# The sync engine holds back context, stores, x and expert weights until a row of maxima has landed

## The chip, the cores and the metric

The kernel runs on one core of one Trainium2 chip. Its time is the device time in microseconds of one execution.
## The reference

32 batches of 112 tokens (width 256) attend with 16 heads to a context of 375 rows, and then pass a mixture of 8 experts of which each token takes 2:

```python
x = x + tanh(g_xattn[0]) * xattn(layernorm(x), ctx, ctx, Wq, bq, Wk, bk, Wv, bv, Wo, bo)
x = x + tanh(g_ffn[0]) * ffn(layernorm(x), w_router, w1, w2, w3)

# xattn: softmax(Q K^T / sqrt(16)) V per head, then Wo, bo
# ffn: scores = softmax(xf @ w_router.T); the 2 best experts of a token;
#      y_e = (silu(xf @ w1[e]) * (xf @ w3[e])) @ w2[e]; sum of score * y_e over the two
```

The context comes in transposed (features first). All is float32; matrix operands are kept as float32r in a few places.

## The kernel before

**Attention** is a pipeline over batches. Every engine runs a loop over `i` from -3 to 31 (SP to 32), and in turn `i` works on several batches at once: exponentials of batch `b = i`, maxima of the scores of `c = i + 1`, value projection of `s = i + 2`, key and query projection of `a = i + 3`, the output projection of `e = i - 1` and the second layer norm of `r = i - 2`. A turn has 12 places `k`, one for each of the 12 score tiles (`exps`, line 1130).

The softmax needs the row maxima before the exponentials. `maxes` (line 1162) computes the scores of batch `c` into PSUM, VectorE takes the negated maxima (line 869), TensorE turns them (`negmax_turn`, line 1178), ScalarE copies them to SBUF (line 645), and GpSimd sends them with two small DMAs (`nm_rows`, line 389) into row 96 of `stack`, as an extra row of the matmul operand. This is done in two halves: half 0 of batch `i + 1` at `k = 5` of turn `i`, needed by `exps` at `k = 0` of turn `i + 1`; half 1 of batch `i` at `k = 1` of turn `i`, needed at `k = 6` of the same turn. `s_nmrow[half][batch % 3]` counts 32 for each pair that has landed. The other user of it is line 644: ScalarE does not overwrite the copied maxima before the send of the batch before has landed.

**The sync engine.** In turn `i`, SP first waits for the low half of the keys of batch `i + 2` (line 298) and then issues 16 DMAs that build that batch's `stack` (lines 280 to 286); the maxima of that batch read it from `k = 0` of turn `i + 1`. Behind them it issues what the turn has left: the context of batch `i + 4` (line 221, read by the key projection at `k = 2` of turn `i + 1`), the store of the attention result of batch `i - 2` (242) and of its norm for batch `i - 3` (248), now and then four batches of x (228), in turns 1 to 6 copies that fill `xn_dram` (320), from turn 3 on expert weights (325). Then it goes on to turn `i + 1`. Turn 1 also fills the table of tokens and some spare rows (315 to 318). SP's order is the order of the code.

**The end of attention.** In turn 30 (`i == LAST - 2`) SP has no stack to build. It issues two stores and then `first_weights` (line 256): 16 transfers of the upper half of `w3` (8, line 261) and of the first rows of `w2` (8, line 263), into memory that `split` and `stack` held. The `n`-th of them waits until `exps` of batch 30 has done `3n/4 + 1` of its 12 tiles (line 258). Then come four `load_idx` (253: the token numbers of the first four expert tiles, read from a table in DRAM), and in turn 31 two stores, the rest of `w2` (line 337, 1024 and 768 KB) and the numbers of 12 more tiles.

**The experts** are 63 tiles of up to 128 tokens. GpSimd gathers a tile's rows by its numbers (`gather`, line 496; the first four in turn 31), TensorE turns them (`turn_rows`, 1361), multiplies by `w1` and `w3` (`inner`, 1417), turns the hidden tile (1436) and multiplies by `w2` (1478); GpSimd adds the result into `out` (505). TensorE waits for the first gathered tile at `k = 10` of turn 31 (line 1337), and for all of `w2` before its first use (line 1472). Tiles turn, gather and add in order of their number.

Of the kernel before, what the change touches and what calls it, by code (L numbers as in the profile page):

```python
# [6 lines left out]
def flamingo(nc, x, ctx_kv, g_xattn, g_ffn, Wq, bq, Wk, bk, Wv, bv, Wo, bo, w_router, w1, w2, w3, out):  # L7
# [4 lines left out]
    B, SQ, EMB = x.shape  # L12
# [12 lines left out]
    NSLOT = 3  # L25
    NX = 16
    GB = 4
    NG = B // GB

    NE, _, F = w1.shape  # L30
    TOK = B * SQ
    TOP = 2
# [15 lines left out]
    with ctx, late:  # L48
# [3 lines left out]
        def sem(name):  # L52
            return ctx.enter_context(nc.semaphore(name))
# [77 lines left out]
        s_nmrow = [[sem(f"s_nmrow{h}{n}") for n in range(NSLOT)] for h in range(2)]  # L131
# [52 lines left out]
        def placed(n, g):  # L184
            return 16 * TOP * sum(len(UNITS[u]) for u in range(g, n, 2))

        def wait(eng, s, v):
            if v > 0:
                eng.wait_ge(s, v)  # L190

        def place_of(n):
            return (n - B) % NSLOT
# [6 lines left out]
        def stacked(n):  # L200
            return 256 * (n // NSLOT + 1) - (96 if n % NSLOT == 0 else 0)

        def live(n):
            return n if 0 <= n < B else None
# [13 lines left out]
        def _(sp):  # L218
            def load_ctx(b):
                wait(sp, s_v_ps, KC * (b - NSLOT + 1))  # L220
                sp.dma_start(ctx_t[:, b % NSLOT, :, :], ctx_kv[b, :, :].rearrange("(c p) s -> p c s", p=P)).then_inc(s_ctx[b % NSLOT], 16)

            def load_x(g):
                if g >= 4:
                    wait(sp, s_xn2, GB * (g - 3))
                    for n in range(GB):
                        wait(sp, s_x2st[n], 16 * (g - 3))
                sp.dma_start(xa[:, GB * g % NX:GB * g % NX + GB, :], x[GB * g:GB * g + GB, :, :].rearrange("b q d -> q b d")).then_inc(s_x[g % 4], 16)
# [11 lines left out]
            def store_x2(b):  # L240
                wait(sp, s_st2, b + 1)
                sp.dma_start(out[SQ * b:SQ * b + SQ, :], xrow(b)).then_inc(s_x2st[b % GB], 16)

            def store_xn2(r):
                if r == GB * (SNAP + 1):
                    sp.wait_ge(s_spare, SPARE)
                sp.wait_ge(s_xn2 if r < B - 1 else s_xn2_end, min(r + 1, B - 1) if r < B - 1 else 1)
                sp.dma_start(xn_dram[SQ * r:SQ * r + SQ, :], xn2[:, r % GB, :]).then_inc(s_xn2st[r % GB], 16)

            def load_idx(t):  # L250
                at = sp.value_load(s_idx[0:1, t:t + 1], min_val=0, max_val=ROWS // P - 1)
                wait(sp, s_idx_in[t % NIS], 16 * (t // NIS))
                sp.dma_start(idx[:, t % NI, :], table.rearrange("(t p) c -> t p c", p=P)[bass.ds(at, 1), :, :].rearrange("t p c -> p (t c)")
                             ).then_inc(s_idx_in[t % NIS], 16)

            def first_weights():
                for n in range(2 * NE):
                    sp.wait_ge(s_exp_ps, 12 * (B - 2) + 3 * n // 4 + 1)
                    e = n % NE
                    if n < NE:  # L260
                        sp.dma_start(w3_hi[:, e, :], w3[e, P:2 * P, :]).then_inc(s_w13, 16)
                    else:
                        sp.dma_start(w2_sb[:, 0, e, :], w2[e, 0:P, :]).then_inc(s_w2, 16)

            for i in range(FIRST, LAST + 1):
                s, a = live(i + 2), live(i + 3)
                if i == LAST - 2:
                    sp.wait_ge(s_map, 1)
                    for g in range(2):
                        sp.wait_ge(s_scat[g], placed(SNAP + 1, g))  # L270
                    sp.sem_inc(s_met_sp, 1)
                if s is not None:
                    if s < 2:
                        sp.wait_ge(s_split0, 1)
                    wait(sp, s_exp_ps, 12 * (s - NSLOT + 1))
                    src, dst = split[:, s % 2, :, :].bitcast(f32), stack[:, place_of(s), :, :].bitcast(f32)

                    def from_high(g):
                        rows, pr = slice(32 * g, 32 * g + 32), slice(DC * g, DC * g + DC)
                        sp.dma_start(dst[0:32, pr, 0:SKP], src[rows, :, KHI:KHI + SKP]).then_inc(s_stack[s % NSLOT], 16)  # L280
                        sp.dma_start(dst[0:32, pr, SKP:KQ], src[rows, :, QHI:QHI + QW]).then_inc(s_stack[s % NSLOT], 16)

                    def from_low(g):
                        rows, pr = slice(32 * g, 32 * g + 32), slice(DC * g, DC * g + DC)
                        sp.dma_start(dst[32:64, pr, :], src[rows, :, KLO:KLO + KQ]).then_inc(s_stack[s % NSLOT], 16)
                        sp.dma_start(dst[64:96, pr, :], src[rows, :, KHI:KHI + KQ]).then_inc(s_stack[s % NSLOT], 16)

                    if s == 0:
                        sp.wait_ge(s_qlo, 1)
                        sp.wait_ge(s_khi, DC)  # L290
                        for g in range(3):
                            from_high(g)
                        sp.wait_ge(s_klo, DC)
                        for g in range(2):
                            from_low(g)
                    else:
                        wait(sp, s_klo, DC * (s + 1))
                        sp.sem_inc(s_met_sp, 1)
                        wait(sp, s_qlo, s + 1)
                        for g in range(4):  # L300
                            from_high(g)
                            from_low(g)
                if a is not None and NSLOT - 1 <= a < B - 1:
                    load_ctx(a + 1)
                if live(i - 2) is not None:
                    store_x2(i - 2)
                if live(i - 3) is not None:
                    store_xn2(i - 3)
                if i == -1:
                    load_x(2)  # L310
                if i == 2:
                    load_x(3)
                if i == 1:
                    sp.wait_ge(s_pad, 2)
                    sp.dma_start(table.rearrange("(p n) c -> p (n c)", n=256), pad_tab[:, :, :, :].rearrange("p a b c -> p (a b c)")).then_inc(s_tab0, 16)
                    for n in range(DC):
                        sp.dma_start(out[TOK:TOK + P, P * n:P * n + P], ident[:, :]).then_inc(s_spare, 16)
                        sp.dma_start(xn_dram[TOK:TOK + P, P * n:P * n + P], ident[:, :]).then_inc(s_spare, 16)
                for n in range(GB * (SNAP + 1) + 2 * i - 2, GB * (SNAP + 1) + 2 * i) if 1 <= i <= (B - GB * (SNAP + 1)) // 2 else ():
                    sp.dma_start(xn_dram[SQ * n:SQ * n + SQ, :], x[n, :, :]).then_inc(s_spare, 16)  # L320
                if i == 3:
                    sp.wait_ge(s_tab0, 16)
                for n in (2 * i - 6, 2 * i - 5) if 3 <= i < 8 else (i + 2,) if 8 <= i < 22 else ():
                    src, dst, h = ((w1, w1_sb[:, 0], 0), (w1, w1_sb[:, 1], 1), (w3, w3_lo, 0))[n // NE]
                    sp.dma_start(dst[:, n % NE, :], src[n % NE, P * h:P * h + P, :]).then_inc(s_w13, 16)
                if i >= 7 and i % GB == 3 and (i + 9) // GB < NG:
                    load_x((i + 9) // GB)
                if i == LAST - 2:
                    sp.wait_ge(s_stack[(B - 1) % NSLOT], stacked(B - 1))
                    first_weights()  # L330
                    for t in range(4):
                        load_idx(t)
                if i == LAST - 1:
                    sp.wait_ge(s_nmrow[1][(B - 1) % NSLOT], 32 * ((B - 1) // NSLOT + 1))
                    for c in range(1, FC):
                        n = min(P, F - P * c)
                        sp.dma_start(w2_sb[0:n, c, :, :], w2[:, P * c:P * c + n, :].rearrange("e p d -> p e d")).then_inc(s_w2, 16)
                    for t in range(4, NI):
                        load_idx(t)
# [1166 lines left out]
```

## Time and profile before

| | us |
|---|---|
| median of 3 runs | 856.07 (853.0 to 857.51) |
| the profiled execution, its own time | 855.32 |
| its span in the trace | 853.6 |
| busy in the span: PE / PEld / DVE / ACT / POOL | 825.3 / 673.7 / 486.3 / 422.2 / 476.2 |
| mean granted clock of TensorE | 0.991 of full speed |

The attention takes the span up to about 570 us, the expert tiles the rest. A busy PE is not PE at its peak, since the ends of matmuls are modelled; whether PE is what others wait for is to be read from the chain of waits and from the idle time in front of its lines. A row of a timeline gives the start, the duration, the engine and the line; SPq is the sync engine's queue, and its duration is that of the issue, not of the transfer. In brackets stands the idle time ahead of an instruction and who ended it. "To landing" is the time from an issue to the last write. A turn of attention takes about 16.9 us.

### The profile page before, as it was taken

How to read it: one execution, taken by the hardware profiler on the slowest of the kernel's cores; microseconds unless marked ns; L12 is line 12 of the kernel's file. 1: busy time of each engine (PE TensorE's matmuls, PEld its weight loads, DVE VectorE, ACT ScalarE, POOL GpSimd, SP SyncE). 2: the span in 40 equal slices, each digit the busy share in tenths (PEclk: the TensorE clock that was granted, in tenths of full speed). 3: DMA queues.
4: the chain of work that ended last, by engine and by line, in shares of the span. 5: the costliest groups of instructions: out<-in, count | busy, mean ns of one | idle time of the engine just before them, and what ended most of it. 6: DMA issues, size and time to landing. Idle time of an engine off the chain costs nothing.

```text
span 853.6 us, 21453 instructions
## 1 busy us (share of the span) xinstructions
PE 825.3 (97%) x7209; PEld 673.7 (79%) x7209; DVE 486.3 (57%) x1163; ACT 422.2 (49%) x1086; POOL 476.2 (56%) x570
## 2 busy tenths in 40 slices
PE   7899999999999999999999999899999999999995
PEld 6578888888888888888888888777777777777773
DVE  4566776777777776777787777655622222222221
ACT  2256665665666566656665666565222222222221
POOL 6454434454555555555655465455777766656652
PEclk8999999999999999999999999999999999999997
DMA  5876777776676677676656664574444443444432
GB/s 153 207 161 168 204 177 174 180 192 156 161 181 155 158 175 172 148 175 164 170 117 158 150 160 111 146 192 74 57 63 62 70 69 62 63 63 63 63 57 31
DMA packets 99842, 112.29 MB, mean 132 GB/s; under 512 B 29276, under 2 KB 81124, under 8 KB 99736
## 3 DMA queue, kind: packets, MB, share of 16 engines
q1 hardware_dynamic: 79720, 92.48, 45.1%
q0 software_dynamic: 18512, 17.60, 13.5%
q8 instruction: 61, 1.00, 0.6%
q10 hardware_dynamic: 1504, 0.85, 0.5%
q14 instruction: 45, 0.37, 0.2%
HBM read 35.48 MB, written 17.53 MB: 62 GB/s over the span
## 4 chain that ended last, share of the span: by engine, by line
PE 85%; DVE 11%; issue 2%; ACT 1%; DMA 1%; POOLq 0%; DVEq 0%; ACTq 0%
PE ps L1417 18%; PE ps L1173 10%; PE ps L1478 10%; PE ps L1162 9%; PE ps L1145 9%; PE ps L1130 8%; DVE negmax L869 6%; PE ps L1168 5%; PE ps L1273 3%; PE ps L1332 3%; PE ps L1436 2%; PE ps L1361 2%; PE ps L1265 2%; PE ps L1247 1%; DVE xa L854 1%
## 5 line engine op out<-in xcount | busy, mean ns | idle before, releaser
L869 DVE TENSOR_REDUCE negmax<-ps 112x2 f32<-112x750 f32 x256 | 240.1, 940 | 124.3 <-PE ps L1162 122.8
L594 ACT ACTIVATE probs<-ps 125x448 f32<-125x448 f32 x384 | 209.5, 547 | 101.8 <-PE ps L1130 95.6
L389 POOL DMA_DIRECT2D stack<-negmax_t x128 | 68.2, 536 | 228.5 <-ACT negmax_t L645 220.8
L1130 PE MATMUL ps<-stack 97*125 97x224 f32 x768 | 189.1, 328 | 0.9 <-ACT probs L594 0.4
L1130 PEld LDWEIGHTS ps<-stack 97*125 97x125 f32 x768 | 127.4, 188 | 28.1 <-ACT probs L594 1.5
L1162 PE MATMUL ps<-stack 96*112 96x376 f32 x512 | 136.7, 348 | 7.7 <-DVE negmax L869 5.4
L505 POOL DMA_INDIRECT out_dram<-y,idx x63 | 100.5, 1595 | 69.5 <-issue 34.4
L689 ACT ACTIVATE silu<-ps 128x352 f32<-128x352 f32 x63 | 29.3, 465 | 184.4 <-PE ps L1417 184.4
L1081 DVE TENSOR_TENSOR h<-silu,ps 128x352 f32<-128x352 f32 x63 | 32.8, 521 | 144.6 <-PE ps L1417 144.4
L1168 PE MATMUL ps<-wv_sb,ctx_t 128*125 128x256 f32 x384 | 100.0, 382 | 0.4 <-DVE split L859 0.4
L1173 PE MATMUL ps<-ctx_t,wk_sb 128*128 128x375 f32 x256 | 93.7, 489 | 0.7 <-ACT q_raw L654 0.7
L1478 PE MATMUL ps<-w_sb,h_t 128*128 x378 | 92.3, 380 | 0.7 <-ACT h_t L695 0.7
L1478 PEld LDWEIGHTS ps<-w_sb,h_t 128*128 128x128 f32 x378 | 71.7, 190 | 20.1 <-issue 0.9
L1417 PE MATMUL ps<-w_sb,xg_t 128*128 x252 | 84.9, 458 | 0.0
L1162 PEld LDWEIGHTS ps<-stack 96*112 96x112 f32 x512 | 72.0, 177 | 15.0 <-DVE negmax L869 13.9
L1145 PE MATMUL ps<-probs,v_sb 125*17 125x112 f32 x3072 | 79.8, 260 | 0.0
L1145 PEld LDWEIGHTS ps<-probs,v_sb 125*17 125x17 f32 x3072 | 71.7, 98 | 8.0 <-ACT probs L594 5.4
L496 POOL DMA_INDIRECT xg<-xn_scratch,idx x63 | 62.5, 992 | 25.4 <-issue 17.2
L567 ACT ACTIVATE v_sb<-ps 125x256 f32<-125x256 f32 x96 | 36.5, 381 | 78.8 <-PE ps L1145 76.6
L409 POOL DMA_INDIRECT slot_table<-pay,slots_i x64 | 64.2, 1003 | 15.3 <-issue 13.6
L1168 PEld LDWEIGHTS ps<-wv_sb,ctx_t 128*125 128x125 f32 x384 | 66.6, 187 | 6.8 <-DVE split L859 0.6
L1173 PEld LDWEIGHTS ps<-ctx_t,wk_sb 128*128 128x128 f32 x256 | 46.7, 195 | 18.3 <-issue 1.7
(221 smaller groups left out, 1216.9 us busy)
## 6 DMA issues: line engine op xcount, KB each, us to landing
stack<-split SPq DMA_DIRECT2D x252, 150.0 KB, 2.7
ctx_t<-in_ctx_dram SPq DMA_DIRECT2D x32, 375.0 KB, 3.9
stack<-split SPq DMA_DIRECT2D x127, 94.0 KB, 2.5
stack<-split SPq DMA_DIRECT2D x127, 56.0 KB, 2.1
out_dram<-xa SPq DMA_DIRECT2D x32, 112.0 KB, 3.5
xn_scratch<-xn SPq DMA_DIRECT2D x32, 112.0 KB, 3.3
xa<-in_x_dram SPq DMA_DIRECT2D x7, 448.0 KB, 5.6
w_sb<-in_L_ffn_w_dram SPq DMA_DIRECT2D x16, 176.0 KB, 3.1
```

The lines of the kernel that those rows point to most:

```text
L389: gp.dma_start(dst[:, :, SKP + SQ * h:SKP + SQ * h + SQ], negmax_t[4 * h:4 * h + 4, half, :].bitcast(f32)).then_inc(s_nmrow[half][c % NSLO ...
L409: gp.indirect_dma_start(table, bass.IndirectOffsetOnAxis(ap=slots_i[:, u % 2, GB * k + j:GB * k + j + 1], axis=0), pay[:, UNITS[u][j], k, ...
L505: gp.indirect_dma_start(out, bass.IndirectOffsetOnAxis(ap=idx[:, t % NI, 0:1], axis=0), y[:, t % NY, :], None, compute_op=ALU.add).then_in ...
L594: act.activation(probs[:, n % NP, :], ps[0:KW, EXPB + k % 2, 0:4 * SQ], ACT.Exp).then_inc(s_exp, 1)
L869: dve.tensor_reduce(negmax[:, half, :, p4], ps[0:SQ, m1:m2 + 1, 0:SK], axis=AX.X, op=ALU.max, negate=True).then_inc(s_max, 1)
L1130: last = pe.matmul(ps[0:KW, EXPB + k % 2, QW * m:QW * m + QW], stack[:, place_of(b), p, KW * ch:KW * ch + KW], stack[:, place_of(b), p, SK ...
L1145: last = pe.matmul(ps[32 * j:32 * j + HD + 1, PVB, SQ * g:SQ * g + SQ], v_sb[:, b % NSLOT, ch, head, :], probs[:, (12 * b + 3 * g + ch) % ...
L1162: last = pe.matmul(ps[0:SQ, max_banks(c, t)[h], 0:SKP], stack[0:ONE_ROW, place_of(c), t, SKP + SQ * h:SKP + SQ * h + SQ], stack[0:ONE_ROW, ...
L1168: last = pe.matmul(ps[0:KW, bank, 0:EMB], ctx_t[:, s % NSLOT, n, KW * ch:KW * ch + KW], wv_sb[:, n, :], start=(n == 0), stop=(n == DC - 1))
L1173: last = pe.matmul(ps[:, bank, 0:SK], wk_sb[:, n, P * m:P * m + P], ctx_t[:, a % NSLOT, n, :], start=(n == 0), stop=(n == DC - 1))
L1417: last = pe.matmul(ps[:, bank, 0:F], xg_t[:, t % NS, k, :], w[k][:, bass.ds(e, 1), :].rearrange("p e f -> p (e f)"), start=(k == 0), stop= ...
L1478: last = pe.matmul(ps[:, YB, 0:EMB], h_t[0:n, c, :], w2_sb[0:n, c, bass.ds(e_o, 1), :].rearrange("p e d -> p (e d)"), start=(c == 0), stop ...
```

## The change

One wait is added to the sync engine's loop, in turns 0 to 30, between the stack transfers and everything else that the turn issues:

```diff
                         for g in range(4):
                             from_high(g)
                             from_low(g)
+                if 0 <= i < B - 1:
+                    sp.wait_ge(s_nmrow[0][(i + 1) % NSLOT], 32 * ((i + 1) // NSLOT + 1))
                 if a is not None and NSLOT - 1 <= a < B - 1:
                     load_ctx(a + 1)
                 if live(i - 2) is not None:
```

The semaphore is that of half 0 of batch `i + 1`. No instruction is added besides, none is removed and none changes its place in a stream. So the order of every engine is as before, and only what an instruction waits for differs. On the sync engine, from the stores of turn 29 to the first of the weights, before:

```order
L242 DMA out_dram<-xa 112x256 [waits s_st2]
L248 DMA xn_scratch<-xn 112x256 [waits s_xn2]
L242 DMA out_dram<-xa 112x256 [waits s_scat1,s_map,s_scat0,s_st2]
L248 DMA xn_scratch<-xn 112x256 [waits s_xn2]
L261 DMA w_hi<-in_L_ffn_w_dram 128x352 [waits s_exp_ps,s_stack1]
```

And the same place now:

```order
L242 DMA out_dram<-xa 112x256 [waits s_st2,s_nmrow00]
L248 DMA xn_scratch<-xn 112x256 [waits s_xn2]
L242 DMA out_dram<-xa 112x256 [waits s_scat1,s_map,s_scat0,s_st2,s_nmrow01]
L248 DMA xn_scratch<-xn 112x256 [waits s_xn2]
L261 DMA w_hi<-in_L_ffn_w_dram 128x352 [waits s_exp_ps,s_stack1]
```

The first row stands behind the stack of turn 29 and the third opens turn 30; `s_nmrow01` is half 0 of batch 31. The same wait stands in front of the context load (line 221) of turns 0 to 27.

## Rows read from the trace of the kernel before

**Rows 1.** The page: the chain that ended last by engine, and line 1130 with its idle time.
```profile
PE 85%; DVE 11%; issue 2%; ACT 1%; DMA 1%; POOLq 0%; DVEq 0%; ACTq 0%
...
L1130 PE MATMUL ps<-stack 97*125 97x224 f32 x768 | 189.1, 328 | 0.9 <-ACT probs L594 0.4
```

**Rows 2.** Timeline, sync engine, one step: start us, us, engine, line, what.
```profile
309.90 0.59 SPq L280 DMA_DIRECT2D stack<-split  x1
...
315.04 1.87 SPq L280 DMA_DIRECT2D stack<-split  x1
...
320.79 0.60 SPq L286 DMA_DIRECT2D stack<-split  x1
321.43 0.59 SPq L221 DMA_DIRECT2D ctx_t<-in_ctx_dram  x1
...
323.08 0.43 SPq L325 DMA_DIRECT2D w_lo<-in_L_ffn_w_dram  x1
326.74 0.61 SPq L280 DMA_DIRECT2D stack<-split  x1
```

**Rows 3.** Timeline, GpSimd, in the same step: the two sends of maxima.
```profile
321.58 1.06 POOL L389 DMA_DIRECT2D stack<-negmax_t  x2 [3.40 <-ACT negmax_t L645]
```

**Rows 4.** Line 389 alone, 321.0 to 321.8 us: time to landing.
```profile
DMA to landing us min/median/max: 3.8/3.8/3.8
```

**Rows 5.** DMA issues, 312 to 329.7 us: KB each, median us to landing.
```profile
stack<-split SPq DMA_DIRECT2D x9, 150.0 KB, 2.7
...
ctx_t<-in_ctx_dram SPq DMA_DIRECT2D x1, 375.0 KB, 4.1
```

**Rows 6.** Timeline, TensorE, the start of the next step.
```profile
328.97 0.46 PE L1130 MATMUL ps<-stack 97*125 97x224 f32 x2
329.55 0.60 PE L1162 MATMUL ps<-stack 96*112 96x376 f32 x2
...
333.32 1.43 PE L1173 MATMUL ps<-ctx_t,wk_sb 128*128 128x375 f32 x4
```

**Rows 7.** Timeline, GpSimd, loop turn 3: the two sends of maxima.
```profile
101.64 1.09 POOL L389 DMA_DIRECT2D stack<-negmax_t  x2 [4.71 <-ACT negmax_t L645]
```

**Rows 8.** Timeline, sync engine, first stack transfers of turns 4 and 5.
```profile
106.82 0.65 SPq L280 DMA_DIRECT2D stack<-split  x1
...
123.66 0.65 SPq L280 DMA_DIRECT2D stack<-split  x1
```

**Rows 9.** Timeline, GpSimd, the end of attention.
```profile
555.97 1.07 POOL L389 DMA_DIRECT2D stack<-negmax_t  x2 [2.03 <-PE ps L1130]
...
564.61 1.08 POOL L496 DMA_INDIRECT xg<-xn_scratch,idx  x1 [0.17 <-issue]
```

**Rows 10.** Line 389 alone, 555.9 to 557 us: time to landing.
```profile
DMA to landing us min/median/max: 2.7/2.8/2.9
```

**Rows 11.** Timeline, sync engine, the end of attention.
```profile
547.68 6.72 SPq L261 DMA_DIRECT2D w_hi<-in_L_ffn_w_dram  x8
555.37 4.22 SPq L263 DMA_DIRECT2D w_sb<-in_L_ffn_w_dram  x8
560.66 4.83 SPq L253 DMA_DIRECT2D idx<-slot_table  x4
...
566.48 1.26 SPq L337 DMA_DIRECT2D w_sb<-in_L_ffn_w_dram  x2
```

**Rows 12.** The same, 548.2 to 549.5 us alone: two issues.
```profile
548.11 0.93 SPq L261 DMA_DIRECT2D w_hi<-in_L_ffn_w_dram  x2
```

**Rows 13.** Timeline, TensorE, first expert tile turned, first use of w2.
```profile
569.81 0.38 PE L1361 MATMUL ps<-ident,xg 128*128 128x128 f32 x2
...
580.45 1.54 PE L1478 MATMUL ps<-w_sb,h_t 128*128 x6
```

**Rows 14.** DMA issues, 561 to 590 us: KB each, us to landing.
```profile
w_sb<-in_L_ffn_w_dram SPq DMA_DIRECT2D x1, 768.0 KB, 12.3
```

**Rows 15.** Stretches: us, busy us of PE, PEld, DVE, ACT, POOL, PEclk, DMA.
```profile
12.00:16.00 4.00, 3.63 (x11) 2.88 (x12) 0.28 (x1) 0.82 (x3) 0.80 (x2) 0.50 0.57 121
```

## The prediction

> **What bounds the kernel now.** I read the page first: the chain of waits that ended last and the costliest lines. The reader is to see that TensorE holds 85% of the chain, VectorE 11% and DMA 1% [rows 1]. The new wait is for a DMA that brings maxima to line 1130, so the second thing to see is the idle time in front of that line: 0.9 us in the whole run, and ended by ScalarE, not by a transfer [rows 1]. No maxima are late now. Then I read the sync engine's timeline, once in the middle of the attention and once at its end, and beside it the sends of the maxima and the readers on TensorE. The end matters because there the sync engine's stream holds something else: the first expert weights, the first token numbers, the rest of w2.
>
> **The added wait in a common turn.** A turn takes 16.84 us, from the stack's first transfer at 309.90 to the next batch's at 326.74 [rows 2]. The stack's 16 issues last to 321.43; then come context, two stores and one weight slice, done at 323.51, and the engine stands idle for 3.2 us [rows 2]. GpSimd sends half 0 at 321.58, two DMAs in 1.06 us, so the second starts at about 322.1 [rows 3], and it takes 3.8 us to land [rows 4]. The wait therefore ends at 325.9 at the latest. What is queued behind it takes 323.51 - 321.43 = 2.1 us, and is out at 328.0: the next stack starts 1.3 us later than 326.74. Who waits for that?
>
> - The context, issued at 325.9 with 4.1 us to landing [rows 5], is there at 330.0. The key projection reads it at 333.32 [rows 6]. Spare: 3.3 us.
> - The stack's last issue, at 320.79 now, lands 2.7 us later at 323.5 [rows 2, 5]; the maxima read it at 329.55 [rows 6]. 6.1 us of spare, 4.8 us after the shift.
> - The sync engine itself: 328.0 plus 11.5 us for the stack (321.43 - 309.90) is 339.5, and the next maxima land at 325.9 + 16.84 = 342.7. It does not fall behind from turn to turn.
> - Stores, x and weights have readers that are at least a turn away.
>
> So I cost the wait at nothing in common turns; what hides it is the 3.2 us in which the sync engine is idle anyway and the 3.3 us by which the context is early. In turn 3 seven DMAs are held (context, two stores, two copies, two weight slices), 7 x 0.53 = 3.7 us at the pitch of the four above. The sends start at 101.64 [rows 7], the second lands at about 102.2 + 3.8 = 106.0, the seven are out at 109.7, and the stack of turn 4 starts 2.9 us after its 106.82 [rows 8]. Of 6.1 us of spare 3.2 us are left. Turns 4 to 6 are alike, turn 1 holds eight small ones.
>
> Does it gain anything? The maxima would no longer have the context transfer beside them. They might land in 2.8 us, as at the end of attention [rows 10], instead of 3.8 us. But they land at 325.9 now and are read at 328.97 [rows 6]; earlier is worth nothing. And the turn with more traffic is not longer: from turn 4 to 5, with two copies and two slices in it, the stack starts are 123.66 - 106.82 = 16.84 us apart [rows 8], as in the middle [rows 2]. The Trainium skill says, in "DMA: Bandwidth & Descriptors", section "Issuing engines are not separate DMA queues", that transfers of all engines interleave on the same 16 DMA engines; by that rule alone holding back the context should speed up the maxima, and the sum would be a gain of up to 1 us a turn if somebody waited for them. The two landing times (3.8 and 2.8 us) agree with it, and the 0.9 us of idle time says that nobody waits.
>
> **The added wait in turn 30.** Here the cover is gone. There is no stack in this turn, so the sync engine comes to the wait early. The sends of half 0 of batch 31 start at 555.97 [rows 9]; the second at 556.5, and it lands 2.8 us later [rows 10], at 559.3. Now the w3 transfers are spread from 547.68 to 554.4 and those of w2 from 555.37 to 559.59, paced by the score tiles, and the first token numbers are issued at 560.66, 1.07 us after the last of them [rows 11]. With the wait, two stores and 16 transfers start at 559.3 together. The pacing no longer delays them, but each issue costs: two in 0.93 us, or 0.48 us each with the gap [rows 12]. 18 x 0.48 = 8.6, so they are out at 567.9, and the first numbers are issued at 569.0, 8.3 us later than now. With no w3 traffic beside them the maxima will land sooner than in 2.8 us; I take off 0.5 us, a choice, and have a shift of 7.8 us for all that follows on the sync engine. Two readers are on the path:
>
> - The first gather. It starts at 564.61 [rows 9], and TensorE turns its tile at 569.81 [rows 13]: at most 5.2 us from gather to tile. The trace does not show its landing, and 2.7 us, a plain transfer's [rows 5], is the least I allow. The numbers issued at 568.5 land 2.7 us later, so the gather starts at about 571.4 and the tile is there between 574.1 and 576.6. TensorE loses 4.3 to 6.8 us.
> - The rest of w2. The second of its two transfers is issued at about 567.2 [rows 11] and takes 12.3 us [rows 14], to 579.5; its first use is at 580.45 [rows 13]. The margin is 0.9 us. Shifted by 7.8 us, it makes TensorE 6.9 us late, the first loss included.
>
> The later of the two decides: 6.9 us. Behind it nothing gives it back, since the expert tiles are TensorE's work back to back. Sum against the profiled execution: 855.3 + 0 (30 turns) + 6.9 = 862.2 us. The median of the three runs is 0.7 us above that execution, well within what they differ by.
>
> The ends of this term: at the pitch of a stack issue, 0.64 us [rows 2], the 18 take 2.9 us more, and a stretched issue such as that of 1.87 us [rows 2] adds 1.3 us, so 866 is reachable; the shift cannot be under what the gather allows with the fastest landing, 3.6 us.
>
> **Rivals.**
>
> - *The tail costs less.* The 12.3 us of w2 are so long because gathers, stores and number loads run beside it [rows 14]; if those are spread differently, w2 arrives sooner, and only the gather counts: 4.3 us less the 0.7 us that the maxima may land earlier, 3.6 us, 858.9 us. For it: margins of a microsecond decide. Against: all its neighbours shift with it.
> - *The clock.* TensorE will stand still for over 4 us, and then 10.6 us of work lie before the first use of w2 (580.45 - 569.81). After the first waits of the kernel the granted clock was 0.50 over 12 to 16 us, the level of 1.2 GHz [rows 15]. If 4 us at that level follow the stop, 2 us are lost, less what the wait for w2 hides (0 to 2.6 us): up to 864.2 us. The Trainium skill, "TensorE: Matmul & The Clock Gate", Part 1, says that an idle array falls back to half rate; what it gives here is that time, and no stop so long is in the attention of this trace.
> - *Slower in the attention.* In turns 1 and 3 to 6 the spare is down to 3.2 us by my count, and the held transfers (about 1.2 MB) lie directly ahead of the stack in the queue. If they cost 5 us instead of 3, TensorE loses 2 us in each of five turns: 872 us. It decides once a stack lands over 6.1 us later than now.
> - *Faster.* A common turn gets shorter because no bulk transfer is beside the maxima, by 0.4 us in each of 30 turns: 12 us, less the tail, 850 us. It decides if line 1130 or its ScalarE readers wait for landings that the trace puts down to others. Against it stand the 0.9 us of idle time and the equal turns.
> - That the wait does nothing is excluded by the rows: the engine reaches it at 321.43, and the landing is at 325.9.
>
> **Chances.** Forecast 0.52 (859.5 to 866), less tail 0.20, clock 0.09, slower attention 0.06, faster 0.13. What a measurement can tell from no change is 0.5%, 4.3 us. Slower by more than that: the forecast, clock and attention, and 0.03 of the less costly tail, 0.70. Within it: the rest of that case, 0.17. Faster: 0.13. The range of 856.5 to 866.5 leaves out the faster case, a little of the cheap tail, and the slow attention. Slower holds most, and the forecast's own range is 859.5 to 866.
>
> **What would show it.** Right: the turns stay at 16.8 us and the context load starts at the landing of the maxima; the w3 and w2 transfers of turn 30 stand in one block from about 559 to 568; the first numbers are issued near 568.5; line 1361 has 4 to 7 us of idle time, ended by the gather, and line 1478 perhaps 1 to 2 us before its first use. Wrong: idle time in front of line 1162 or 1173 ended by a DMA in the attention, or a block of 16 transfers that is out before 565, or turns under 16.6 us.

## The result and the profile after

| | before | now |
|---|---|---|
| median of 6 runs, us | 856.79 (853.0 to 858.1) | 862.96 (862.31 to 865.86) |
| ratio of the times, 95% interval | | 1.0091 (1.006 to 1.0122) |
| the profiled execution, its span, us | 855.32, 853.6 | 862.31, 860.6 |
| mean granted clock of TensorE | 0.991 | 0.990 |

The kernel is slower by 0.9%, or 6.2 us of the medians. The forecast was 862.2 us.

The page first: the shares of the chain, and the line that reads the maxima.

```profile
PE 84%; DVE 11%; issue 2%; DMA 2%; ACT 1%; SPq 0%; ACTq 0%; POOLq 0%; POOL 0%; DVEq 0%
...
L1132 PE MATMUL ps<-stack 97*125 97x224 f32 x768 | 189.3, 329 | 2.9 <-DMA stack<-negmax_t 2.1
```

Against [rows 1] TensorE has one point less and DMA one more, and line 1132 (1130 before) now waits 2.9 us instead of 0.9, ended by the landing of maxima. The waits of the sync engine (total us, times, longest) show where the added wait acts:

```profile
SPq L221 <- DMA stack<-negmax_t: 69.8, 28, 5.0
SPq L298 <- DVE split L861: 19.2, 19, 2.3
SPq L242 <- DMA stack<-negmax_t: 15.5, 3, 11.3
```

28 waits in front of the context and 3 in front of line 242, the longest of them 11.3 us: that one is turn 30. A common turn now, on the sync engine:

```profile
318.04 0.60 SPq L286 DMA_DIRECT2D stack<-split  x1
321.44 0.40 SPq L221 DMA_DIRECT2D ctx_t<-in_ctx_dram  x1
...
322.85 0.46 SPq L327 DMA_DIRECT2D w_lo<-in_L_ffn_w_dram  x1
324.49 0.61 SPq L280 DMA_DIRECT2D stack<-split  x1
```

This turn stands 2.25 us earlier in the trace than the one of [rows 2], for a reason that lies at the start of the kernel and is told below. The context goes out 3.4 us after the stack's last issue began, and the next stack starts at 324.49. With 2.25 added that is 326.74, the very time of [rows 2]: it is not late at all. Over turns 2 to 27 the context goes out 2.1 to 3.4 us after the first send of half 0 (once 4.6 us), and in turns 3 to 8 the next stack starts 0.7 to 1.7 us later than before. From the first value matmul of turn 1 to that of turn 30 the attention takes 489.85 us now and took 489.88 before.

From there to the end it is 313.83 us instead of 304.56, 9.3 us more. First the sync engine at the end of the attention, then GpSimd, then the landing of GpSimd's second pair of sends, those of half 1 of batch 31:

```profile
555.86 0.33 SPq L242 DMA_DIRECT2D out_dram<-xa  x1
556.24 0.42 SPq L248 DMA_DIRECT2D xn_scratch<-xn  x1
556.76 3.74 SPq L261 DMA_DIRECT2D w_hi<-in_L_ffn_w_dram  x8
560.54 4.95 SPq L263 DMA_DIRECT2D w_sb<-in_L_ffn_w_dram  x8
566.55 3.68 SPq L253 DMA_DIRECT2D idx<-slot_table  x4
...
571.22 1.30 SPq L339 DMA_DIRECT2D w_sb<-in_L_ffn_w_dram  x2
```

```profile
553.70 1.07 POOL L391 DMA_DIRECT2D stack<-negmax_t  x2 [2.03 <-PE ps L1132]
...
559.77 1.03 POOL L391 DMA_DIRECT2D stack<-negmax_t  x2 [3.62 <-ACT negmax_t L647]
...
569.99 1.08 POOL L498 DMA_INDIRECT xg<-xn_scratch,idx  x1 [7.81 <-DMA idx<-slot_table]
```

```profile
DMA to landing us min/median/max: 4.3/5.0/5.7
```

For comparison the same pair in the kernel before:

```profile
DMA to landing us min/median/max: 1.9/2.4/2.8
```

The two stores and the 16 weight transfers stand in one block from 555.86 to 565.5, the first numbers follow at 566.55, and the gather waits 7.81 us for them. New is what the landings show: the pair sent at 559.77, behind w3 and beside w2, lands after 4.3 to 5.7 us instead of 1.9 to 2.8. TensorE, the readers and the first use of w2, and the landing of its last part:

```profile
566.01 0.70 PE L1132 MATMUL ps<-stack 97*125 97x224 f32 x4 [2.11 <-DMA stack<-negmax_t]
...
573.42 0.41 PE L1363 MATMUL ps<-ident,xg 128*128 128x128 f32 x2 [2.46 <-DMA xg<-xn_scratch,idx]
...
578.90 3.42 PE L1147 MATMUL ps<-probs,v_sb 125*17 125x112 f32 x96
...
587.61 1.54 PE L1480 MATMUL ps<-w_sb,h_t 128*128 x6
```

```profile
w_sb<-in_L_ffn_w_dram SPq DMA_DIRECT2D x1, 768.0 KB, 12.2
```

TensorE stands still twice, 2.11 us for the maxima and 2.46 us for the first gathered tile; in front of its first use of w2, at 587.61, it does not wait. The last part of w2, issued at about 571.9, landed at 584.1. And the stretches of this place (columns as in [rows 15]):

```profile
560.00:566.00 6.00, 3.43 (x76) 2.72 (x64) 3.30 (x18) 2.40 (x5) 2.14 (x4) 1.00 1.00 342
566.00:570.00 4.00, 3.77 (x15) 2.97 (x16) 0.18 (x2) 2.46 (x6) 0.01 (x1) 0.65 0.27 74
570.00:574.00 4.00, 1.54 (x11) 1.18 (x10) 1.25 (x4) 0.68 (x2) 3.09 (x4) 0.92 0.58 163
574.00:578.00 4.00, 3.90 (x17) 2.36 (x15) 0.65 (x5) 2.44 (x7) 3.35 (x4) 0.50 1.06 309
578.00:582.00 4.00, 3.72 (x94) 3.27 (x98) 0.00 (x0) 0.41 (x1) 0.63 (x1) 0.64 0.97 180
```

The granted clock is 0.50 to 0.92 from 566 to 582 us; in the trace of before every stretch from 549 to 600 has 1.00. Both kernels take the same 253.60 us from a later point to the end (from 607.00 now, from 600.00 before), so the 9.3 us arise ahead of it. The stretches from the value matmuls of turn 30 to that point, now and before:

```profile
546.77:607.00 60.23, 52.98 (x520) 41.21 (x520) 25.85 (x92) 29.51 (x65) 29.81 (x31) 0.91 0.49 117
```

```profile
549.04:600.00 50.96, 48.59 (x521) 38.57 (x521) 25.93 (x93) 29.43 (x65) 29.67 (x31) 1.00 0.59 133
```

The same work (520 and 521 recorded matmuls) takes 60.23 us instead of 50.96. TensorE is busy 52.98 us of it instead of 48.59: 4.4 us more for the same instructions, at a clock of 0.91. The other 4.9 us are more idle time.

These two sums do not say which stop decides, and the order of events does. The first tile is turned 26.65 us after turn 30's value matmuls (573.42 - 546.77) and was turned 20.77 us after them before (569.81 - 549.04): 5.9 us late. The tile hangs on the numbers, and these on the sync engine's issues, which do not wait for half 1. So the stop of 2.11 us, and the lower clock of the stretch behind it, lie inside this lateness: without them TensorE would have waited longer for the same tile. From the tile to the first use of w2 it is then 14.19 us instead of 10.64, 3.5 us more, with TensorE busy for 13.81 us of them at a mean granted clock of 0.76. These two terms, 5.9 and 3.5 us, make the 9.3, give or take 0.1.

Against these 9.3 us stand 2.3 us that were won before turn 1. The added wait is first met in turn 0, so it has no part in them. The first rows of TensorE's timeline, now and before:

```profile
1.61 9.15 PE L1119 MATMUL ps<-ident 128*128 128x128 f32 x56 [1.61 <-POOL ident L366]
...
13.31 2.70 PE L1175 MATMUL ps<-ctx_t,wk_sb 128*128 128x375 f32 x8
```

```profile
1.61 7.99 PE L1117 MATMUL ps<-ident 128*128 128x128 f32 x56 [1.61 <-POOL ident L364]
...
14.18 4.95 PE L1173 MATMUL ps<-ctx_t,wk_sb 128*128 128x375 f32 x8
```

The same 56 warm-up matmuls took 9.15 us in this execution and 7.99 us in the other, so that TensorE stood still for 0.65 us behind them here and for 1.81 us there; the first 8 key projections then took 2.70 us at a granted clock of 1.00, and 4.95 us at the 0.50 of [rows 15]. Executions differ there without an edit, as the runs below show (with the same warm-up the value matmuls of turn 1 start between 56.9 and 59.8 us). So 7.0 us between the two spans are 9.3 lost at the end of the attention less 2.3 won at the start.

### The profile page after: what moved, and what is told of

Same layout as the page of the kernel before. It is cut to its first block, busy times and chain, and to the rows that moved or that the text cites. A ratio compares the mean times of both kernels' runs of the same rounds, so it can differ in the third digit from the quotient of the medians.

```text
span 860.6 us, 21484 instructions
## 1 busy us (share of the span) xinstructions
PE 827.7 (96%) x7209; PEld 675.7 (79%) x7209; DVE 486.3 (57%) x1163; ACT 422.1 (49%) x1086; POOL 476.1 (55%) x570
## 3 DMA queue, kind: packets, MB, share of 16 engines
q0 software_dynamic: 18512, 17.60, 12.8%
## 4 chain that ended last, share of the span: by engine, by line
PE 84%; DVE 11%; issue 2%; DMA 2%; ACT 1%; SPq 0%; ACTq 0%; POOLq 0%; POOL 0%; DVEq 0%
PE ps L1419 17%; PE ps L1480 10%; PE ps L1164 9%; PE ps L1175 9%; PE ps L1147 9%; PE ps L1132 8%; DVE negmax L871 6%; PE ps L1170 5%; PE ps L1275 3%; PE ps L1334 3%; PE ps L1438 2%; PE ps L1363 2%; PE ps L1267 1%; PE ps L1249 1%; DVE xa L856 1%
## 5 line engine op out<-in xcount | busy, mean ns | idle before, releaser
L1175 PE MATMUL ps<-ctx_t,wk_sb 128*128 128x375 f32 x256 | 91.5, 479 | 0.7 <-ACT q_raw L656 0.7
L1419 PEld LDWEIGHTS ps<-w_sb,xg_t 128*128 128x128 f32 x252 | 47.9, 191 | 17.2 <-issue 0.5
```

The lines of the kernel that those rows point to most:

```text
L1175: last = pe.matmul(ps[:, bank, 0:SK], wk_sb[:, n, P * m:P * m + P], ctx_t[:, a % NSLOT, n, :], start=(n == 0), stop=(n == DC - 1))
L1419: last = pe.matmul(ps[:, bank, 0:F], xg_t[:, t % NS, k, :], w[k][:, bass.ds(e, 1), :].rearrange("p e f -> p (e f)"), start=(k == 0), stop= ...
```

## The experiments

In all of them "the wait" is the added one. Turn lengths are the distances between the first value matmuls of neighbouring turns; "the tail" is the time from turn 30's to the end of the span, 304.56 us before and 313.83 now. Unless an edit says otherwise it is made to the changed kernel.

**The wait in turns 0 to 29 alone**, and **in turn 30 alone**:

```diff
-                if 0 <= i < B - 1:
+                if 0 <= i < B - 2:      # the first kernel
+                if i == B - 2:          # the second
```

> The added wait stands in turns 0 to 29 only. Theory (all of the loss is made in turn 30, the wait in a common turn is hidden): no change, ratio 1.000 within 0.002; the turns after turn 2 stay at 16.85 to 17.15 us as in the kernel before, and from the value matmuls of turn 30 to the end of the span it is 304.6 us as before. Rival 1 (the wait shortens common turns, and the changed kernel got its 2.27 us lead at turn 30 from it): about 2 us faster than before, ratio 0.997. Rival 2 (late stack transfers cost in turns 3 to 6): turns over 17.2 us there.

> The added wait stands in turn 30 only. Theory: it makes the whole loss; from the value matmuls of turn 30 to the end of the span 313.8 us as in the changed kernel, against 304.6 us before, and a ratio of 1.009 like the whole change. Rival (the wait of common turns costs or gains too): the ratio differs from that of the whole change by over 0.002.

Measured: turns 0 to 29 alone 856.68 us (12 runs, 855.01 to 859.32; ratio to before 1.0011, 0.9997 to 1.0024), attention 489.79 us, tail 305.87. Turn 30 alone 862.96 us (6 runs, 860.79 to 866.18; ratio 1.0086, 1.0063 to 1.0108), attention 489.80 us, tail 313.19. So thirty of the 31 waits cost nothing that can be told from noise, and the last one costs all. The tail of the first is 1.3 us over the 304.6 expected: TensorE waits 1.16 us there for the second gathered tile. The same stop, 0.81 us, stands in the kernel before with more warm-up (below), which has no added wait. With turn 30's wait alone TensorE stands still at the same two places:

```profile
568.02 1.07 PE L1132 MATMUL ps<-stack 97*125 97x224 f32 x4 [1.70 <-DMA stack<-negmax_t]
...
575.49 0.66 PE L1363 MATMUL ps<-ident,xg 128*128 128x128 f32 x2 [2.10 <-DMA xg<-xn_scratch,idx]
```

**The first numbers ahead of the weights**, with the full wait. The four `load_idx` of turn 30 go in front of `first_weights`:

```diff
-                    first_weights()
                     for t in range(4):
                         load_idx(t)
+                    first_weights()
```

> The whole change, but in turn 30 the first four token-number loads are issued ahead of the 16 weight transfers, right behind the wait. Theory (three things make the 9.3 us: half 1 of batch 31's maxima behind the weight block, 2.1 us; the late gather, 2.5 us of idle time; the clock that falls after them): the gather starts before 565 us, the wait for it is gone, that of 2.1 us before line 1132 stays or grows by up to 1 us, since the weight block is later by the four number loads of 1.2 us each; total loss 3 to 6 us against before. Rival (the rest of w2 binds behind the gather, as the prediction had it): the loss stays near 7 us, with idle time ahead of the first use of w2.

Measured: 863.25 us (4 runs, 862.37 to 865.29; ratio 1.0095, 1.0072 to 1.0118), tail 313.92. The sync engine, the landing of half 1, and TensorE's idle time over 1 us:

```profile
558.56 4.25 SPq L253 DMA_DIRECT2D idx<-slot_table  x4
562.85 3.78 SPq L261 DMA_DIRECT2D w_hi<-in_L_ffn_w_dram  x8
```

```profile
DMA to landing us min/median/max: 1.9/2.3/2.7
```

```profile
571.95 1.45 PE L1419 MATMUL ps<-w_sb,xg_t 128*128 x4 [2.24 <-DMA w_hi<-in_L_ffn_w_dram]
...
586.74 2.76 PE L1480 MATMUL ps<-w_sb,h_t 128*128 x6 [3.67 <-DMA w_sb<-in_L_ffn_w_dram]
```

The gather starts at 563.16 and no reader of maxima waits, but nothing is won. The half-1 pair, sent at 560.58 with no weight ahead of it, lands in 2.3 us. TensorE then waits 2.24 us for w3, which is issued 5.3 us later than in the changed kernel (15.27 us behind the first value matmul of turn 30 instead of 9.99), and 3.67 us for the last part of w2. The expectation had the stop for half 1 staying and a loss of 3 to 6 us; both were wrong, and its rival, the rest of w2, was right. The first tile is turned 20.77 us after turn 30's value matmuls, just as before.

**The same, and the first part of w2 after half 1.** In `first_weights`:

```diff
+                    if n == NE:
+                        sp.wait_ge(s_nmrow[1][(B - 1) % NSLOT], 32 * ((B - 1) // NSLOT + 1))
```

> As the one before, and the first of the eight w2 transfers of turn 30 waits until half 1 of batch 31's maxima has landed. Theory: the maxima have at most the eight w3 transfers ahead of them, the wait before line 1132 is under 0.5 us, TensorE never stands over 1 us in turn 31, the clock stays at 1.00, and the kernel is within 1 us of the one before. Rival (w2 is what binds next): the w2 block is out near 569 us and the rest of w2 lands near 585 us, so that 3 to 5 us of idle time stand ahead of its first use.

Measured: 862.82 us (5 runs, 862.4 to 864.72; ratio 1.0095, 1.0076 to 1.0114), tail 313.10. The added wait held nothing back: w2 is issued at 566.50, right behind w3, where it was 566.68 without the wait. So this is in effect the kernel ahead of it once more. Idle time before w3's reader is 0.96 us here, and the last part of w2 binds more:

```profile
585.00 2.92 PE L1482 MATMUL ps<-w_sb,h_t 128*128 x6 [4.80 <-DMA w_sb<-in_L_ffn_w_dram]
```

**Only that: w2 after half 1**, with the numbers behind the weights as in the change.

> The whole change, and in turn 30 the first of the eight w2 transfers waits until half 1 of batch 31's maxima has landed; the token numbers stay behind the weights. Theory: the 2.1 us of idle time before line 1132 is gone or under 0.5 us, the gather is later than in the changed kernel by 0 to 3 us and TensorE waits 4 to 7 us for it, so the loss stays at 7 to 10 us. Rival (the loss at line 1132 is not due to the weight block in front of the maxima): the idle time there stays at 2.1 us.

Measured: 865.89 us in one run, span 864.2, tail 314.95, with the turn ahead of turn 30 1.6 us longer than before's besides, for which no edit was made. The half-1 pair still takes 4.4 us to land and the stop for it is 1.35 us, so w3 alone is enough to delay it (the expectation had under 0.5 us of stop), and the wait for the first tile grows to 5.47 us, since the numbers now stand behind one wait more.

**Turn 30 waits for half 1 of batch 31** instead (no wait in other turns). The block of weights then cannot be ahead of that pair.

```diff
-                if 0 <= i < B - 1:
-                    sp.wait_ge(s_nmrow[0][(i + 1) % NSLOT], 32 * ((i + 1) // NSLOT + 1))
+                if i == B - 2:
+                    sp.wait_ge(s_nmrow[1][(B - 1) % NSLOT], 32 * ((B - 1) // NSLOT + 1))
```

> The added wait stands in turn 30 only and is for half 1 of batch 31's maxima, so that not one weight transfer is issued before it has landed. Theory (in the changed kernel half 1 landed late because the block of weights was ahead of it): its two sends land in 1.9 to 2.6 us instead of 4.3 to 5.7, no idle time ahead of the 7th score tile of turn 31; everything on the sync engine is some 5 us later than in the changed kernel, so TensorE stands 7 to 9 us for the first gathered tile, and the span from turn 30's value matmuls to the end is 317 to 321 us. Rival (half 1 lands late for another reason): the sends still take 4 us or more.

Measured: 867.74 us in one run, span 866.0, tail 318.31. The landing of half 1, and the first tile on TensorE:

```profile
DMA to landing us min/median/max: 1.9/2.2/2.6
```

```profile
579.48 0.66 PE L1363 MATMUL ps<-ident,xg 128*128 128x128 f32 x2 [10.85 <-DMA xg<-xn_scratch,idx]
```

The block now starts at 564.68, the pair is sent at 560.69, lands in 2.2 us, and nobody waits for it. The stop for the first tile is longer than the 7 to 9 us expected. The tile is 11.0 us late (31.79 us after the value matmuls, 20.77 before), and 2.8 us more are lost from there to the first use of w2, at a mean granted clock of 0.78: together the 13.8 us by which this tail is longer than before's. Together with the kernel that sends the numbers first, it shows what delayed half 1: the weights issued ahead of it.

**TensorE kept busy in turn 31.** 16 transposes of the identity at `k = 6` and 20 ahead of the first expert tile, into PSUM that is free there:

```diff
+                    if i == B - 1 and k == 6:
+                        pe.wait_ge(s_max, 8 * B)
+                        for n in range(16):
+                            pe.transpose(ps[:, MAXB, P * (n % 4):P * (n % 4) + P], ident[:, :], ident[:, :])
...
+                        for n in range(20):
+                            pe.transpose(ps[:, XTB, P * (n % 4):P * (n % 4) + P], ident[:, :], ident[:, :])
                         turn_rows(0)
```

> The changed kernel, and TensorE does work without use in turn 31: 16 transposes of the identity ahead of the score tile that waits for half 1 of the maxima, 20 ahead of the first gathered tile. Theory (the clock cost some 3 us of the 9.3 us: after the stops the granted clock was 0.50 to 0.65 for about 14 us): the granted clock stays at 1.00 from 566 to 582 us, the transposes fit into the idle time, and from the value matmuls of turn 30 to the end of the span it is 310 to 311.5 us, against 313.8 in the changed kernel. Rival (the clock cost nothing that the waits did not hide): 313.8 us or more.

Measured: 862.67 us (6 runs, 859.18 to 865.54; ratio 1.0065, 1.0043 to 1.0087). The profiled execution was the slowest of the six, 865.54 us, tail 314.03. Its stretches:

```profile
566.00:574.00 8.00, 7.48 (x58) 6.65 (x58) 3.43 (x16) 4.34 (x10) 1.08 (x1) 1.00 0.51 158
574.00:578.00 4.00, 2.13 (x22) 1.81 (x21) 0.23 (x3) 1.18 (x5) 2.88 (x4) 0.96 0.85 228
578.00:582.00 4.00, 3.33 (x14) 1.46 (x18) 0.50 (x4) 1.80 (x3) 3.12 (x3) 0.50 1.09 276
582.00:586.00 4.00, 4.00 (x98) 3.55 (x91) 0.00 (x0) 0.34 (x1) 0.00 (x0) 0.69 0.84 150
```

The clock is full up to 574 and falls later, behind a stop of 1.78 us in front of the first tile. The expected tail did not come in this profile: the first tile was turned 26.55 us after turn 30's value matmuls, against 26.65 in the changed kernel, though nothing stood still for half 1 and the clock was full up to there. This bears out that the stop for half 1 and the clock behind it cost nothing by themselves, since the gather decides when the tile is there. Over the runs the granted clock was 0.988 to 0.996 (mean 0.992) where the changed kernel had 0.983 to 0.990 (mean 0.986), and the filled kernel's three runs with 0.994 to 0.996 (859.18, 860.37 and 861.85 us) are below every run of the changed kernel. But the intervals of the two ratios overlap. That the clock's share can be had back in this way is supported, not shown.

**Where the spare of a common turn ends.** No wait for maxima; instead turns 0 to 28 hold the same transfers until TensorE has got to a given score tile; the semaphore is the one that counts the finished score tiles of `exps`:

```diff
-                if 0 <= i < B - 1:
-                    sp.wait_ge(s_nmrow[0][(i + 1) % NSLOT], 32 * ((i + 1) // NSLOT + 1))
+                if 0 <= i < B - 3:
+                    sp.wait_ge(s_exp_ps, 12 * i + 12)   # the first kernel; 13 in the second
```

> In turns 0 to 28 the sync engine holds context, stores, x and weights not until half 0 has landed but until the last score tile of the turn (the 12th of batch i), some 3 us later; no added wait in turns 29 and 30. Theory (3.3 us of spare of the context, 4.8 us of the stack): the common turn stays at 16.85 to 17.15 us, the context load starts near the end of the turn. Rival (the spare is less than the rows of before say): turns get longer by up to 2 us.

> As the one before, but until the first score tile of the next turn, a further 1.1 us. The context is then issued at about 0.3 us after the start of the next turn's first score tile and needs 3.6 to 4.1 us, and its reader comes 4.3 us after that start. Theory: the edge of the spare; turns longer by 0 to 1.5 us, with idle time ahead of the key projection (line 1175) ended by the context transfer. Rival (the spare is larger, since other things hide it): no longer turn at all; rival 2: stack transfers are late first, and the idle time stands ahead of line 1164.

Measured, held to the last tile of the turn: 858.94 us in one run, attention 490.87 us (one turn of 18.12 us, in which TensorE waits 1.00 us for a row of maxima, all others as before). Held to the first tile of the next turn: 866.41 us in one run, attention 498.91 us, with five turns of 17.57 to 18.12 us and one of 20.03 where before has 16.8 to 17.6, and the last two before turn 31 together 4 us longer. What TensorE waits for there (total us, times, longest):

```profile
PE ps L1164 <- DMA stack<-split: 5.8, 5, 1.8
```

It is the stack that comes late, and never the context; once, for 0.84 us, maxima do. Four of the five stops lie in common turns, and in these the last transfer of the stack was issued 12.8 to 13.8 us after the first value matmul of its turn, where before it was mostly 7 to 8. TensorE needs the stack at 14.7 us, for the first maxima tile of the next batch, so a last issue later than about 12.0 us makes it wait; with the 2.7 us to landing of [rows 5] that closes. The first of the two kernels showed something else. Its tail is 308.56 us, 4 us over before's, though its end of attention is the old one: in turn 31 no stop is longer than 0.98 us, and yet

```profile
560.00:566.00 6.00, 5.05 (x113) 4.26 (x113) 2.44 (x14) 3.08 (x10) 3.85 (x6) 1.00 0.35 69
566.00:576.00 10.00, 9.85 (x40) 7.73 (x39) 3.77 (x20) 5.91 (x14) 5.62 (x6) 0.53 0.98 238
```

So the clock can fall in turn 31 without a wait added there, and the tail was 4 us longer when it did. The high busy time of the second row comes with the fall, since each matmul takes longer at the lower clock. The kernel before was not profiled in such an execution; of 23 timed executions of it three took 859.30 to 860.23 us at a granted clock of 0.986 to 0.990, and the median was 855.68.

**Ten more warm-up matmuls**, in the kernel before, and **these with three transposes ahead of five of the tiles of turn 31**:

```diff
-        WARM = 56
+        WARM = 66
...
+                    if i == B - 1 and k in (1, 3, 5, 7, 9):     # the second kernel
+                        if k == 1:
+                            pe.wait_ge(s_max, 8 * B)
+                        for n in range(3):
+                            pe.transpose(ps[:, MAXB, P * (n % 4):P * (n % 4) + P], ident[:, :], ident[:, :])
```

> The kernel before, with 66 instead of 56 transposes of the identity at the start of TensorE. Theory (in the traces TensorE stood 1.81 us between these and the first matmul of the kernel where the granted clock was 0.50 in 12 to 16 us, and 0.65 us where it was not; the difference at turn 1 was 2.24 us): the clock stays at 1.00 until turn 1, which starts at 56.9 to 57.8 us, in every run; median 1 to 2 us under that of before, ratio 0.998 to 0.999. Rival (the clock of the start is not set by that gap): turn 1 at 57.7 to 59.4 us as before, ratio 1.000.

> The same, and in turn 31, in which TensorE is busy for only some 80% of the time and in some traces falls to a granted clock of 0.50 without a long stop, 3 transposes of the identity ahead of each of five score tiles. Theory (the spread of the kernel before comes from this drop too): the low runs near 853 us become the rule, the median is 2 to 3 us under that of before, ratio 0.997. Rival (the added 15 transposes, some 2 us, are not hidden): ratio 1.000 or more, turn 31 longer than 11.4 us by up to 2 us.

Measured: 855.15 us (12 runs, ratio 0.9988, 0.9968 to 1.0007) and 854.57 us (12 runs, ratio 0.9992, 0.9977 to 1.0008). Neither can be told from before. In the first, turn 1 started at 60.02 us, later than before, at a granted clock of 0.91 between 20 and 57 us. The first key projections took 2.71 us there, at the full clock, so the stretch of 12 to 16 us was mended; but the clock fell later, to 0.50 from 36 to 40 us. More warm-up does not make the start sure. No version was found that beats both kernels.

## Why the prediction came out

**Common turns at nothing: right.** Turns 0 to 29 alone give no difference, and the turns are the old ones to 0.03 us. The working was on the safe side twice. It let the maxima take the 3.8 us of [rows 4]; with no context beside them they land in 1.5 to 1.7 in the turn shown, and in under 3 in all turns but one. And it had the next stack 1.3 us late; it is not late at all, because the four held DMAs are out at 323.31 and the stack waits for the keys anyway. For turn 3 it had 2.9 us, and the trace has 105.77 + 2.25 - 106.82 = 1.2 us. The spare of 6.1 us for the stack was misread, though. [rows 6] start at the second tile (`k = 1`) of the turn; the first one and the first reader of the new stack stand just ahead of them in the trace of before:

```profile
327.44 0.46 PE L1130 MATMUL ps<-stack 97*125 97x224 f32 x2
327.73 0.51 PE L1162 MATMUL ps<-stack 96*112 96x376 f32 x2
```

The stack that lands at 323.5 is read at 327.73 and has 4.2 us of spare, and the maxima that land at 325.9 are read at 327.44 and have 1.5. In turn 3 the forecast shift of 2.9 us would have left 1.3 us, not 3.2. The conclusion held because the shifts were small against 4.2 us too; the holding kernels find the edge there, and not at 6.1. The earlier landing gained nothing, since nobody waited for it, as the 0.9 us of [rows 1] had said.

**The block of turn 30: right.** 18 issues were to take 8.6 us and all behind them to come 7.8 us later. Set beside before's trace (2.27 us added) they went out from 558.1 to 567.8, where the working had 558.8 to 567.4; the 16 weights alone took 8.7 us, and the first numbers came 566.55 + 2.27 - 560.66 = 8.2 us later.

**The first gather: right.** Its tile was to be there at 574.1 to 576.6; it was at 573.42 + 2.27 = 575.7, 5.9 us late.

**"The rest of w2 decides", 6.9 us: wrong for this kernel.** This is the step on which the sum stood. Its last part landed at 584.1, which is 586.4 in the time of before's trace and 5.9 us behind the first use there, not 6.9. That is just as late as the tile, so at the full clock the two would have met, with hardly a wait. Behind the low clock TensorE came to w2 3.5 us later still, 587.61 + 2.27 - 580.45 = 9.4 us late, and did not wait for it. That the margin is as thin as it was put ([rows 11, 13, 14]: 0.9 us) is shown by the kernels with the numbers first, where TensorE gets to w2 earlier and waits 3.67 and 4.80 us for it; the use is then 586.74 + 1.46 - 580.45 = 7.8 us late (that execution reached turn 30 1.46 us earlier than before's), where 6.9 were forecast.

**What the working lacked: half 1 of batch 31.** The prediction named two readers behind the block and missed a third that is not on the sync engine at all. GpSimd's sends of half 1 start 3.0 us after the first weight is issued, and share the DMA engines with 2.4 MB that used to be spread over 12 us. TensorE stands 2.11 us for them, but in this kernel that stop adds nothing to the time: it lies ahead of the first tile, which would not have been there sooner. The prediction weighed the Trainium skill's "DMA: Bandwidth & Descriptors", section "Issuing engines are not separate DMA queues", only for common turns, where interleaving on the same 16 engines could speed the maxima up. The same rule works the other way in turn 30, and there the trace has its number: 5.0 us instead of 2.4.

**The clock, held at 0.09 and at most 2 us: it came, and cost 3.2 us.** The working let the clock fall only behind a stop of over 4 us. It was under full for most of the 16 us from 566 to 582, from the stop of 2.11 us on and again behind the one of 2.46 us (the price of the lower level: 8 projections take 4.95 us at the 0.50 of [rows 15], and 2.70 us at the full clock). Of the 4.4 us of added busy time the part ahead of the first tile is covered by the gather; behind it TensorE is busy for 13.81 us where it was for 10.64, and no wait for w2 hides any of that. The Trainium skill, "TensorE: Matmul & The Clock Gate", Part 1, says that an idle array falls back to half rate; here the array fell also in the kernel whose longest stop in that turn was 0.98 us, so stops alone do not tell it.

**The sum.** 862.2 us stand against 862.31 of the profiled execution, and that closeness is luck. The end of the attention cost 9.3 us, not 6.9, and the profiled execution had started 2.3 us better than the one of before. And the 9.3 are not made of the term that was forecast: they are 5.9 us of the gather, rightly sized but taken for the lesser of the two, and 3.5 us at a low clock, which the sum put at nothing. The medians are 6.2 us apart, and the fastest executions, 862.31 and 853.0 us, 9.3. Direction, place and the size of the block were right by their reasons; the 6.9 was not. Why it did not help to take one reader out of the way: the gather, w3, half 1 and w2 all have only a few microseconds to spare, and the stream now ends some 8 us later. Take one stop away and the next deadline in the row takes its place: with the numbers first, the medians were still 863.25 and 862.82 us.

What stays open: how much of the 3.5 us of clock belongs to the change. The clock falls in some executions of kernels with the old end of attention too, and the medians suggest less than the profile.

## What to carry to other kernels

A wait that is added to an in-order queue costs nothing while the queue has idle time behind it and what it holds has spare; count both per turn, and then look at the turn in which the queue holds something else, for there the same line can cost everything. Paced transfers that are let go at once may also delay small transfers of other engines that fall behind them. And where several deadlines lie within a few microseconds of each other, mending one shows only the next: shorten the stream ahead of all of them, or leave the wait out of that turn.

## What the runs showed of the hardware

- Sends of 1.8 KB by GpSimd landed in 1.5 to 1.7 us in a turn of the changed kernel with no context load beside them; before, one landed 3.8 us after its issue beside such a load [rows 4]. Behind and beside 16 weight transfers of 2.4 MB two took 4.3 to 5.7 us, and a median of 4.4 us behind 8 of them.
- An issue of a weight transfer on the sync engine takes 0.47 us (3.74 us for 8), and 0.62 us on average in the second half of the block (4.95 us for 8, one of them 1.52 us).
- The last part of w2, 768 KB, took 12.2 us to land here, 12.3 before [rows 14], and 14.3 in the kernel with the numbers first.
- The granted clock of TensorE fell, to a mean of 0.53 over 10 us, behind 6 us in which it had been busy for 5.05 with no stop over 0.98 us. Kernels with the old end of attention had tails from 304.56 to 308.56 us.
